# Own keys of the causal maxima in banks of their own, masked by GpSimd instead of by a matmul

## The reference

```python
q = (rmsnorm(h @ wq_a.T, ln) @ wq_b.T).reshape(B, S, 32, 128)   # 64 without position, 64 rotated
kv = rmsnorm(ckv, ln2) @ wkv_b.T                                 # keys and values from 32 latents
q_pe, k_pe = rope(deinterleave(q_pe)), rope(deinterleave(k_pe))
scores = einsum('bqhd,bkhd->bhqk', q_full, k_full) * softmax_scale
scores = where(causal, scores, finfo.min)
attn = softmax(scores, axis=-1)
out = einsum('bhqk,bkhd->bqhd', attn, v).reshape(B, S, 32 * 128) @ wo.T
```

## Time and profile before

| | |
|---|---|
| time, median of 3 runs | 814.38 us (813.57 to 815.26) |
| profiled execution | 814.78 us, its span 812.6 us |
| PE busy | 764.8 us (94%), 3901 matmuls |
| DVE busy | 551.6 us (68%) |
| ACT busy | 275.2 us (34%) |
| POOL busy | 152.5 us (19%) |
| maxima reduced, L1159 | 304 reductions, 194.3 us of DVE |
| mask products of the maxima, L600 | 176, 45.0 us as the page counts them |

### The profile page before, as it was taken

One profiled execution on the slowest core, in us unless ns is written; L12 is line 12 of the kernel. 1 busy time (PEld: TensorE's weight loads), 2 busy tenths in 40 slices (PEclk: granted clock), 3 DMA queues, 4 the chain that ended last, 5 costly groups with the idle time before them and its releaser, 6 DMA issues.

```text
span 812.6 us, 10341 instructions
## 1 busy us (share of the span) xinstructions
PE 764.8 (94%) x3901; PEld 496.5 (61%) x3901; DVE 551.6 (68%) x847; ACT 275.2 (34%) x394; POOL 152.5 (19%) x132
## 2 busy tenths in 40 slices
PE   3898899999999999999999999998997999999997
PEld 1755465555555555555555555443786788886886
DVE  6777579889789889889889879689565222223342
ACT  3732133333333333333333333444243222222210
POOL 1135413113113113113113100010242000000111
PEclk9999899999999999999999999999998999999999
DMA  8333513313213213213213290253000132210011
GB/s 310 151 78 78 133 39 78 71 24 78 70 25 79 68 27 78 67 28 79 66 29 77 52 328 36 105 190 96 1 1 0 46 110 77 78 30 0 27 40 39
DMA packets 36145, 60.72 MB, mean 75 GB/s; under 512 B 4257, under 2 KB 16289, under 8 KB 34305
## 3 DMA queue, kind: packets, MB, share of 16 engines
q1 hardware_dynamic: 36096, 60.06, 26.5%
HBM read 32.66 MB, written 2.10 MB: 43 GB/s over the span
## 4 chain that ended last, share of the span: by engine, by line
PE 62%; DVE 23%; issue 10%; POOL 3%; ACT 2%; DMA 1%; POOLq 0%; SPq 0%; DVEq 0%; ACTq 0%
PE PS L753 15%; DVE PR L1256 7%; PE PS L596 6%; PE PS L659 6%; PE PS L674 6%; PE PS L723 6%; PE PS L660 5%; PE PS L661 5%; DVE NMa L1159 4%; DVE NMb L1159 3%; PE PS L586 3%; PE PS L612 2%; PE PS L663 2%; PE PS L600 1%; POOL OT L1540 1%
## 5 line engine op out<-in xcount | busy, mean ns | idle before, releaser
L890 ACT ACTIVATE PR<-PS 128x1024 f32<-128x1024 f32 (+1 forms) x144 | 132.9, 929 | 255.2 <-PE PS L661 240.2
L1159 DVE TENSOR_REDUCE NMa<-PS 128x1 f32<-128x512 f32 (+3 forms) x216 | 138.9, 663 | 46.2 <-PE PS L600 40.6
L596 PE MATMUL PS<-KH,Q 96*128 96x512 f32 (+3 forms) x384 | 131.3, 401 | 3.0 <-DVE TQ L1144 1.5
L659 PE MATMUL PS<-Q,KH 97*128 97x512 f32 x288 | 131.2, 456 | 0.0
L753 PE MATMUL PS<-Q 128*128 128x512 f32 (+1 forms) x528 | 122.9, 395 | 5.1 <-DVE Q L1355 4.5
L753 PEld LDWEIGHTS PS<-Q 128*128 128x128 f32 (+1 forms) x528 | 99.2, 188 | 28.2 <-DVE Q L1355 4.7
L1256 DVE TENSOR_TENSOR PR<-PR 128x2048 f32<-128x2048 f32 (+3 forms) x56 | 109.3, 1952 | 7.5 <-ACT PR L890 6.4
L660 PE MATMUL PS<-Q,KL 96*128 96x512 f32 x288 | 114.3, 397 | 0.0
L661 PE MATMUL PS<-Q,KH 96*128 96x512 f32 x288 | 113.5, 394 | 0.0
L596 PEld LDWEIGHTS PS<-KH,Q 96*128 96x128 f32 x384 | 67.7, 191 | 57.6 <-issue 35.4
L659 PEld LDWEIGHTS PS<-Q,KH 97*128 97x128 f32 x288 | 55.8, 194 | 32.0 <-issue 13.7
(11 more groups left out here) (177 smaller groups left out, 957.1 us busy)
## 6 DMA issues: line engine op xcount, KB each, us to landing
Q<-TQ SPq DMA_DIRECT2D x64, 384.0 KB, 6.0
RT<-in_wo SPq DMA_DIRECT2D x4, 1024.0 KB, 4.8
TQ<-in_wo SPq DMA_DIRECT2D x4, 1024.0 KB, 5.1
WI<-in_gate_w SPq DMA_DIRECT2D x10, 256.0 KB, 3.3
WI<-in_up_w SPq DMA_DIRECT2D x10, 256.0 KB, 3.6
DI<-in_down_w SPq DMA_DIRECT2D x10, 256.0 KB, 3.8
PR<-in_wmod_c SPq DMA_DIRECT2D x2, 1024.0 KB, 6.4
x_in<-in_x SPq DMA_DIRECT2D x8, 256.0 KB, 9.6
```

The source lines that it names most:

```text
L596: ins = pe.matmul(bank[:, i * w:(i + 1) * w], M.Q[0:KR, g % 2, 0, qt // 4, h0 + i, qs], M.KH[0:KR, lo:lo + w], start=(i == 0), stop=(i == ...
L659: pe.matmul(dst, M.KH[0:KR + 1, ks], M.Q[0:KR + 1, w % 2, 0, qb, :, qs], start=True, stop=False)
L890: act.activation(tiles, banks, ACT.Exp).then_inc(S_.p, 1)
L1159: dve.tensor_reduce(dst, PS[:, bank_of(turn), 0:n * w].rearrange("p (h k) -> p h k", k=w), axis=AX.X, op=ALU.max, negate=True).then_inc(S_ ...
```

## The change

The parts are cut otherwise. For each query tile its **own** 128 keys, for all four heads, make one bank (four matmuls of 128 columns), and the keys before them make the other banks. There are still 38 banks per group: 8 of own keys and 30 others, 22 of 512 columns and 8 of 384. They go by query tile, all heads of one tile together. No part has a mask product. ACT copies the own-key bank to one of two SBUF tiles (`diag`) and so frees it, POOL masks the tile in place with a select, and DVE reduces it later (`least`), in general three banks behind. The results go to `NMd`, and `join` takes one more minimum.

To make room `RE` is no longer a tile of its own but rows 0 and 3 of `RT`: POOL rotates in place, and DVE's next `even` waits until `split_low` has read them. `HANDED` is gone: DVE does group 1's queries like all others. `WV` loads into a place of its own. Two more fills at the start set `NMa` and `NMb`.

By the new table, in windows 0 to 5 the own-key banks are filled in units 1, 1, 3, 5, 8, 13, 17 and 26 (window 0 has the last in 25), the reductions of the masked tiles stand at units 3, 4, 5, 7, 12, 15, 21 or 22, and 28, and join and rows stand at unit 30, behind the last part. In POOL's queue the select of query tile 7 stands behind `split_low` of the second half. In window 6 the join stays at unit 28 and the rows at 30.

```diff
-        for lo in range(0, (qt + 1) * P, 512):
-            w = min(512, (qt + 1) * P - lo)
+        parts.append((qt, qt * P, P, 0, HG))
+        for lo in range(0, qt * P, 512):
+            w = min(512, qt * P - lo)
             n = 512 // w
             parts += [(qt, lo, w, h, n) for h in range(0, HG, n)]
-    return sorted(parts, key=lambda part: (part[0] >= NS // 2, part[3] + part[4]))
+    return parts
...
+LEAST_BEHIND = 3
 def maxima_places(begin, end):
-    cost = [0.14 + w * n / 960 for _, _, w, _, n in PARTS]
-    places = [(begin + (end - begin) * sum(cost[:k]) / sum(cost), ("part", k), cost[k]) for k in range(len(PARTS))]
+    cost = [0.35 if is_diagonal(k) else 0.14 + PARTS[k][2] * PARTS[k][4] / 960 for k in range(len(PARTS))]
+    diagonals = [k for k in range(len(PARTS)) if is_diagonal(k)]
...
+            if k == min(d + LEAST_BEHIND + 1, (diagonals + [len(PARTS)] * 2)[qt + 2]):
+                places.append((at(k), ("least", qt), 0.65))
+        places.append((at(k), ("part", k), 0.0 if is_diagonal(k) else cost[k]))
...
-                            M.KH[0:KR, lo:lo + w], start=(i == 0), stop=(i == n - 1 and not diagonal))
-        if diagonal:
-            corner = bank[:, 0:n * w].rearrange("p (h k) -> p h k", k=w)[:, :, w - P:]
-            ins = pe.matmul(corner, M.identb[:], M.maskb[:].unsqueeze(1).broadcast_to([P, n, P]), start=False, stop=True)
+                            M.KH[0:KR, lo:lo + w], start=(i == 0), stop=(i == n - 1))
...
+    def diagonal_copied(g, k):
+        qt = PARTS[k][0]
+        turn = TURN[("part", g, k)]
+        if NS * g + qt >= 2:
+            act.wait_ge(S_.dm, NS * g + qt - 1)
+        act.wait_ge(S_.side, turn + 1)
+        act.activation(M.diag[:, qt % 2].rearrange("p h k -> p (h k)"), PS[:, bank_of(turn), :], ACT.Copy).then_inc(
             S_.free[turn % 3], 1)
...
         if half > 0:
-            dve.wait_ge(S_.re, 2 * half)
+            dve.wait_ge(S_.tl, half)
...
+    def diagonal_reduced(g, qt):
+        dve.wait_ge(S_.ds, NS * g + qt + 1)
+        dve.tensor_reduce(M.NMd[:, qt // 4, :, qt % 4], M.diag[:, qt % 2], axis=AX.X, op=ALU.max,
+                          negate=True).then_inc(S_.dm, 1)
...
-        dve.tensor_tensor(M.NMa[:, 1], M.NMa[:, 1], M.NMb[:], ALU.min).then_inc(S_.nm, 1)
+        dve.tensor_tensor(M.NMa[:, 1], M.NMa[:, 1], M.NMb[:], ALU.min).then_inc(S_.nj, 1)
+        dve.wait_ge(S_.nj, g + 1)
+        dve.wait_ge(S_.dm, NS * (g + 1))
+        if g > 0:
+            dve.wait_ge(S_.side, TURN[("rows", g - 1)] + 1)
+        dve.tensor_tensor(M.NMj[:], M.NMa[:], M.NMd[:], ALU.min).then_inc(S_.nm, 1)
...
     def rotate(g, hf):
-        half = 2 * g + hf
         for kind in ("even", "odd"):
             pool.wait_ge(S_.free[TURN[(kind, g, hf)] % 3], freed((kind, g, hf)))
-        pool.wait_ge(S_.tl, half)
-        pool.tensor_tensor(M.RE[:, 0, :], M.RT[:, 0, :], M.RT[:, 1, :], ALU.subtract).then_inc(S_.re, 1)
-        pool.tensor_tensor(M.RE[:, 1, :], M.RT[:, 2, :], M.RT[:, 3, :], ALU.add).then_inc(S_.re, 1)
...
+        pool.tensor_tensor(M.RT[:, 0, :], M.RT[:, 0, :], M.RT[:, 1, :], ALU.subtract).then_inc(S_.re, 1)
+        pool.tensor_tensor(M.RT[:, 3, :], M.RT[:, 2, :], M.RT[:, 3, :], ALU.add).then_inc(S_.re, 1)
+
+    def diagonal(g, k):
+
+        qt = PARTS[k][0]
+        tile = M.diag[:, qt % 2]
+        pool.wait_ge(S_.free[TURN[("part", g, k)] % 3], freed(("part", g, k)))
+        pool.affine_select(out=tile, in_=tile, compare_op=ALU.is_ge, fill=MASKED, base=0, pattern=[[0, HG], [-1, P]],
+                           channel_multiplier=1).then_inc(S_.ds, 1)
```

More of the change, by code:

```diff
@@ L197, in __init__ @@
         self.RT = take("RT", [P, 4, 512])
-        self.RE = take("RE", [P, 2, 512])
+        self.diag = take("diag", [P, 2, HG, P])
+        loaded = self.at
         self.WP = take("WP", [P, 2 * P])
@@ L210, in __init__ @@
         self.c_rows = take("c_rows", [P, D])
+        self.NMa = take("NMa", [P, 2, HG, NS // 2])
+        self.NMb = take("NMb", [P, HG, NS // 2])
+        self.NMd = take("NMd", [P, 2, HG, NS // 2])
+        self.NMj = take("NMj", [P, 2, HG, NS // 2])
         self.at = wide
@@ L242, in __init__ @@
         assert self.at <= big
-        self.at = folded
+        self.at = loaded
+        self.WVF = take("WV", [P, 2 * D])
         self.floor = take("floor", [P, 2, D])
@@ L320 @@
 SLACK = 0.04
+LEAST_BEHIND = 3
 def maxima_places(begin, end):
-    cost = [0.14 + w * n / 960 for _, _, w, _, n in PARTS]
-    places = [(begin + (end - begin) * sum(cost[:k]) / sum(cost), ("part", k), cost[k]) for k in range(len(PARTS))]
+    cost = [0.35 if is_diagonal(k) else 0.14 + PARTS[k][2] * PARTS[k][4] / 960 for k in range(len(PARTS))]
+    diagonals = [k for k in range(len(PARTS)) if is_diagonal(k)]
+    at = lambda k: begin + (end - begin) * sum(cost[:k]) / sum(cost)
+    places = []
+    for k in range(len(PARTS)):
+        for qt, d in enumerate(diagonals):
+            if k == min(d + LEAST_BEHIND + 1, (diagonals + [len(PARTS)] * 2)[qt + 2]):
+                places.append((at(k), ("least", qt), 0.65))
+        places.append((at(k), ("part", k), 0.0 if is_diagonal(k) else cost[k]))
     return places + [(end + 0.02, ("join",), 0.1), (end + 0.07, ("rows",), 0.3)]
 def group_places(g, places):
-    return [(place, (name[0], g) + name[1:], 0.0 if name[0] in ("even", "odd") and g in HANDED else busy)
-            for place, name, busy in places]
+    return [(place, (name[0], g) + name[1:], busy) for place, name, busy in places]
 def window_table(w):
@@ L591, in maxima_part @@
         bank = side_bank(TURN[("part", g, k)])
-        diagonal = (qt + 1) * P == lo + w
         qs = slice(qt % 4 * P, qt % 4 * P + P)
@@ L605, in maxima_rows @@
         pe.wait_ge(S_.nm, g + 1)
-        pe.transpose(bank[0:HG * NS, 0:P], M.NMa[:].rearrange("p f h n -> p (f h n)"), M.ident[:]).then_inc(S_.side, 1)
+        pe.transpose(bank[0:HG * NS, 0:P], M.NMj[:].rearrange("p f h n -> p (f h n)"), M.ident[:]).then_inc(S_.side, 1)
     def denominator(w, qb):
@@ L692, in pe_program @@
         side(key)
-    pe.wait_ge(S_.mask, 4)
+    pe.wait_ge(S_.mask, 6)
     pe.wait_ge(S_.one, 1)
@@ L838, in weights_high @@
         act.activation(M.WH[:], M.WF[:], ACT.Copy).then_inc(S_.wh, 1)
-    def queries_copied(kind, g, hf):
-        turn = TURN[(kind, g, hf)]
+    def diagonal_copied(g, k):
[3 more added lines that the diff above has]
+            act.wait_ge(S_.dm, NS * g + qt - 1)
         act.wait_ge(S_.side, turn + 1)
-        act.wait_ge(S_.re, 2 * (2 * g + hf))
-        act.activation(M.RT[:, ("even", "odd").index(kind), :], PS[:, bank_of(turn), :], ACT.Copy).then_inc(
+        act.activation(M.diag[:, qt % 2].rearrange("p h k -> p (h k)"), PS[:, bank_of(turn), :], ACT.Copy).then_inc(
             S_.free[turn % 3], 1)
-    def latent_high(g, hf):
-        turn = TURN[("lat", g, hf)]
-        cols = slice(hf * 512, hf * 512 + 512)
-        for h in range(HG):
-            act.wait_ge(S_.q[hf][h], 16 * g)
-        act.wait_ge(S_.side, turn + 1)
-        act.activation(M.TQ[:, 2, 0, cols], PS[:, bank_of(turn), :], ACT.Copy).then_inc(S_.lh, 1)
     def split_high(g, hf):
@@ L865, in side @@
             weights_high(key[1])
-        elif key[0] in ("even", "odd") and key[1] in HANDED:
-            queries_copied(key[0], key[1], key[2])
-        elif key[0] == "lat" and key[1] in HANDED:
-            latent_high(key[1], key[2])
         elif key[0] == "split":
             split_high(key[1], key[2])
+        elif key[0] == "part" and is_diagonal(key[2]):
+            diagonal_copied(key[1], key[2])
     def exponentials(w, e):
@@ L1136, in latent @@
         cols = slice(hf * 512, hf * 512 + 512)
-        if g not in HANDED:
-            if g > 0:
-                for h in range(HG):
-                    dve.wait_ge(S_.q[hf][h], 16 * g)
-            dve.wait_ge(S_.side, turn + 1)
-            dve.tensor_copy(M.TQ[:, 2, 0, cols], PS[:, bank_of(turn), :]).then_inc(S_.lh, 1)
+        if g > 0:
+            for h in range(HG):
+                dve.wait_ge(S_.q[hf][h], 16 * g)
+        dve.wait_ge(S_.side, turn + 1)
+        dve.tensor_copy(M.TQ[:, 2, 0, cols], PS[:, bank_of(turn), :]).then_inc(S_.lh, 1)
         dve.wait_ge(S_.lh, 2 * g + hf + 1)
@@ L1218, in side @@
             weights_folded(g, key[2])
-        elif kind == "even" and g not in HANDED:
+        elif kind == "even":
             even(g, key[2])
-        elif kind == "odd" and g not in HANDED:
+        elif kind == "odd":
             odd(g, key[2])
@@ L1226, in side @@
             split_low_first(key[2])
-        elif kind == "part":
+        elif kind == "part" and not is_diagonal(key[2]):
             part_reduced(g, key[2])
+        elif kind == "least":
+            diagonal_reduced(g, key[2])
         elif kind == "join":
@@ L1492, in side @@
             weights_low(g)
-        elif kind == "even" and g in HANDED:
-            rotate_even(g, key[2])
-        elif kind == "odd" and g in HANDED:
```

(3 more changed lines are left out.)

51 lines of the change are left out of this document (16 added, 35 removed).

## The result

The changed kernel takes **841.53 us** (median of 4 runs, 840.18 to 845.65) against 814.23 for the kernel before on the same chip: ratio 1.034, 95% interval 1.0324 to 1.0357. Slower was right; 27 us is nine times the 3.0 of my sum and lies above the whole range.

A forecast was written before the change was run, and what follows sets the result against it. PE and DVE were taken to bound the kernel in turn; windows 0 to 5 (+2.8), window 6 (-0.8) and the first maxima (+1.0) gave +3.0 us on the median of 814.38: 817.4 us, range 806.5 to 825.5.

The forecast's parts named there:

- The frame: Windows: up to unit 12 a cheaper PE shortens the window, from there to the join only a cheaper DVE.
- rival 4: PE's clock falls at the rows after a longer wait: 2.0 us in each of six windows, 829 or more; chance 0.05.
- PE: Mask products out, short matmuls in: PE wins 0.8 us per group, booked as -0.4 per window, -0.8 in window 6.
- Select: GpSimd's select of query tile 7 holds off DVE's add or reduction: 0.86 us, +0.86 in windows 0 to 5.
- Reduction from SBUF: DVE's eight reductions per group that now read SBUF: no difference taken from the 681 ns from PSUM.
- rival 2: DVE's reductions from SBUF are cheaper: 805 at the floor, 814.4 at a quarter; 0.22 no change, 0.06 somewhat faster.
- Gap before the denominators: A masked tile's reduction fills DVE's 1.51 us gap there: -0.6 per window, in windows 0 to 5.
- Join and rows: Moved from unit 32 to 30 in windows 0 to 5, with PE's units 31 and 32 still ahead: +0.6 per window.
- ACT copies: Eight copies per group at 0.59 us, behind their unit's exponential on an engine with room: booked at nothing.
- First maxima: Before window 0: group 1's query work returns to DVE, mostly into its gaps: +1.0, bounds 0.3 shorter to 6.3 longer.
- Rival 1: PE's gain arrives whole in units 13 to 30, ACT freeing banks sooner: 803.4 to 810 us; chance 0.24.
- Rival 3: The ring ACT, GpSimd, DVE is too slow for two buffers; one late 1 us turn per window gives 824; chance 0.07.

The follow-up runs named there:

- before_rows_early: Kernel before, with only join and rows moved to unit 30 in windows 0 to 5, behind the last part; 829.16 us, ratio 1.0201.
- before_by_tile: Kernel before, with only its parts put in the order of query tiles, not sorted by head; 815.05 us, ratio 1.0013.
- rows_filler: Changed kernel plus six filler products of 512 columns ahead of PE's wait for the join; 830.54 us, ratio 1.0192.
- rows_late: Changed kernel with join and rows put back to unit 32 in windows 0 to 5; 833.13 us, ratio 1.0224.
- after_join_early: Changed kernel with the join left at unit 30 and the rows alone put back to unit 32; 832.62 us, ratio 1.0224.
- part_filler: Changed kernel plus one filler product of 512 columns ahead of each own-key bank of the windows; 838.21 us, ratio 1.0286.
- join_early_filler: after_join_early plus one filler product of 512 columns ahead of each own-key bank in the windows; 823.83 us, ratio 1.0117.
- ring_out: Changed kernel without ACT copies and selects: own-key banks get a mask product and DVE reduces them from PSUM; 841.65 us, ratio 1.0328.
- mixed_order: Changed kernel with own-key banks spread among long matmuls over each window, join at unit 30, rows at 32; 821.25 us, ratio 1.0089.
- mixed_late_busy: mixed_order with join and rows both at unit 32 and a filler behind every bank ahead of window 0; 821.83 us, ratio 1.0111.

## Why the prediction was wrong

**The frame** was right: PE and DVE in turn, with no gain to be had from masks on PE alone. Without falls the sum comes close: 61.70 us against 61.5 for windows 1 to 5, 52.6 against 52.3 for window 6. Part of that is luck. The select was booked at +0.86 us and did not lengthen the add beside it over that of the kernel before, and the order by tile, which the sum did not have, costs 0.4 us per window in the kernel before.

**The step that failed is the clock.** The sum booked it at nothing, and rival 4 had one fall per window at 0.05. I had both of its inputs: PE's wait at the transpose would grow from 1.0 to 1.8 us (it is 1.58), and 2.83 us had left the clock at 0.5. Between 1.0, harmless, and 2.83, harmful, 1.58 lay open, and I gave it 1 in 20 with no row that spoke for that. before_rows_early shows it lost at 1.48 in five windows of six. Its price I put at 2.0 us; measured is about 1.6 (3.15 for two). And I did not ask what taking PE's work away does to the clock at all. Mask products had stood between the matmuls of units 1 to 5; with them gone and more short matmuls there, the second fall came. Which of the two it takes is not shown. Together: five windows 3.15 us each, window 0 about 1.6, the first maxima 4.5, and 0.95 behind window 7, where half clock lasts longer, some 23 of the 26.7 us. The last of these is not the change's doing: that part is as long in before_by_tile (250.2 us).

How the two falls were shown: the one behind the rows by three runs that remove it (rows_filler, rows_late, after_join_early) and one that makes it in the old kernel. The one in units 3 to 5 by part_filler and join_early_filler, which remove it, though their fillers add columns and shorten a wait at once; no run made it in the old kernel. Not the order and not sixteen short matmuls are enough alone, the ring is not needed (ring_out) and neither is a wait (mixed_order), and the mask products in ring_out did not prevent it. Which mix of short matmuls and folds it takes stays open; so does why equal windows differ.

**The terms**, one by one:
- *PE.* Matmuls of 128 columns start 0.12 us apart (eight from 295.67 to 296.61), near the 0.13 of the earlier trace rows. That PE wins little per group was right too: window 6, where PE leads, got 0.5 us of the 0.8.
- *Select.* 0.645 us, below the 0.86 taken and inside the bounds (0.59 to 1.16). I had added up the price from the 128-element one; the copy's row was nearer. It stretches the add by 0.24, and that add is still shorter than before (2.52 against 2.78), so the 0.86 did not come.
- *Reduction from SBUF.* 672 ns against 681 from PSUM: no difference, as booked, and rival 2 is refuted. By an estimate from the cycle counts of the Trainium skill (VectorE: DVE Perf Modes, The TRN2 errata) it would be some 65 ns shorter; the trace does not agree. Nor are these reductions stretched by GpSimd's products beside them: 673 to 678 ns where one runs. The Trainium skill (SBUF — State Buffer, Who interferes with whom) says that a tensor_reduce never contends with GpSimd; the trace agrees.
- *Gap before the denominators.* It shrank from 1.51 to 0.33 us (in window 3), more than the 0.6 booked, but gaps of 0.3 and 0.5 opened around it, so that the sum stayed near.
- *Join and rows.* +0.54 against +0.6, apart from the clock.
- *ACT copies.* Booked at nothing; PE's second fold waits 0.36 us for one (300.83). The windows without falls have the same wait, and in after_join_early they are no longer than those of the kernel before with the same join, so it adds nothing to them. The rotation in place was hidden, as booked: DVE's product at 329.81 in window 3 waits 0.47 us for PE, not for `split_low`.
- *First maxima.* Apart from the clock +0.6, where +1.0 was booked, but not for the reason given. I took most of DVE's 6.3 us as hidden in its gaps; at equal order and clock 5.0 of them came (mixed_late_busy against before_by_tile), and the order by tile, which I had not counted, gave 4.4 back in the kernel before, part of it by the clock (0.92 there, 1.00 in before_by_tile). The clock there I had booked as a possible gain; it became the larger loss.

**The rivals.** Rival 1 (PE's gain whole) is refuted by after_join_early: at full clock the windows equal those of the kernel before with the same join. Rival 3 (a slow ring) by ring_out and the same run. Rival 4 named the mechanism and one of its two places.
